# Attention with a running state: folding the state by two parity-scaled ScalarE copies instead of one masked VectorE product

## What is computed

```python
def step(carry, xs):                 # over chunks; q, k after elu+1
    S, z = carry
    qc, kc, vcc = xs
    scores = jnp.einsum('bhid,bhjd->bhij', qc, kc) * mask
    num = jnp.einsum('bhij,bhje->bhie', scores, vcc) + jnp.einsum('bhid,bhde->bhie', qc, S)
    den = scores.sum(-1) + jnp.einsum('bhid,bhd->bhi', qc, z)
    out = num / jnp.clip(den, EPS)[..., None]
    S = S + jnp.einsum('bhjd,bhje->bhde', kc, vcc)
    z = z + kc.sum(2)
...
output = gate * memory_output + (1.0 - gate) * local_output
return x + output @ w_o.T + ffn(xn)
```

## Time and profile before

| | us |
|---|---|
| median of 3 runs | 720.18 |
| lowest and highest | 718.6, 721.35 |
| the profiled execution's own time | 717.36 |
| its span (first to last instruction) | 715.4 |

### The profile page before, as it was taken

The page is one execution under the profiler, slowest core; times in us unless marked ns, Lnnn a source line. Parts: engine busy times, 40 slices in busy tenths (PEclk is TensorE's granted clock), DMA queues, the critical chain, the costliest instruction groups (busy, mean ns, idle before and its releaser), DMA issues. The chain is left out here.

```text
span 715.4 us, 23762 instructions
## 1 busy us (share of the span) xinstructions
PE 616.5 (86%) x8674; PEld 511.4 (71%) x8674; DVE 489.7 (68%) x1317; ACT 349.4 (49%) x870; POOL 309.8 (43%) x401
## 2 busy tenths in 40 slices
PE   1988979979966799999999768888888888988885
PEld 1777868868855699999999756666666666656663
DVE  3565556645683356666666548888888887988886
ACT  4438538547434234444444334555555555555442
POOL 1064083171270820000000033777777776777775
PEclk9999999999988689999999958999999999999997
DMA  8044445345245733333343360222522252323120
GB/s 292 33 140 175 162 148 217 113 170 217 69 169 204 259 104 118 112 121 117 111 124 118 106 227 10 63 92 65 190 88 92 61 212 62 92 62 91 33 62 30
DMA packets 59726, 88.20 MB, mean 123 GB/s; under 512 B 8236, under 2 KB 46348, under 8 KB 58604
## 3 DMA queue, kind: packets, MB, share of 16 engines
q1 hardware_dynamic: 50700, 69.43, 28.8%
q0 software_dynamic: 6656, 16.86, 6.8%
q10 hardware_dynamic: 2272, 0.53, 0.3%
HBM read 46.54 MB, written 40.24 MB: 121 GB/s over the span
## 5 line engine op out<-in xcount | busy, mean ns | idle before, releaser
L1628 POOL TENSOR_TENSOR tick_a<-lane 128x1 f32<-128x1 f32 x32 | 6.3, 196 | 155.4 <-POOLq L826 153.1
L1631 POOL DMA_INDIRECT yg<-d_grouped_y,from_row x64 | 63.3, 990 | 15.5 <-issue 11.6
L87 PE MATMUL e_up<-wb,xb 128*128 x144 | 53.8, 373 | 0.7 <-issue 0.7
L1479 ACT ACTIVATE hid<-a_ring,b 64x128 f32<-64x128 f32 x32 | 11.6, 363 | 87.3 <-remote 50.8
L973 ACT ACTIVATE hb<-e_h 88x256 fp32r<-88x256 f32 x72 | 27.4, 380 | 54.3 <-PE e_h L948 54.3
L1462 ACT ACTIVATE with_mem<-a_ring 128x340 f32<-128x340 f32 x128 | 47.1, 447 | 12.2 <-PE a_ring L1320 12.2
L87 PE MATMUL e_y<-wd,hb 88*128 x146 | 49.3, 338 | 1.6 <-DVE hb L1012 1.6
L1005 DVE TENSOR_TENSOR h_sb<-e_up,silu 128x176 f32<-128x176 f32 x72 | 24.6, 341 | 36.5 <-ACT silu L968 36.5
L813 POOL TENSOR_TENSOR ticks<-lane 128x1 f32<-128x1 f32 x4 | 2.2, 562 | 106.3 <-DVE slot_i L731 106.3
L88 PE MATMUL e_up<-wb,xb 128*128 x144 | 47.5, 330 | 0.0
L89 PE MATMUL e_up<-wb,xb 128*128 x144 | 47.5, 330 | 0.0
(11 more groups left out here) (281 smaller groups left out, 2051.2 us busy)
## 6 DMA issues: line engine op xcount, KB each, us to landing
xg<-d_rows SPq DMA_DIRECT2D x77, 128.0 KB, 2.0
d_grouped_y<-y_sb SPq DMA_DIRECT2D x73, 128.0 KB, 1.8
d_v<-v_half SPq DMA_DIRECT2D x8, 544.0 KB
v<-d_v SPq DMA_DIRECT2D x4, 1088.0 KB, 8.8
d_q<-halves SPq DMA_DIRECT2D x8, 512.0 KB
d_k<-halves SPq DMA_DIRECT2D x8, 512.0 KB
skT<-d_k SPq DMA_DIRECT2D x8, 512.0 KB
total<-d_base SPq DMA_DIRECT2D x8, 512.0 KB
```

What stands on the lines that cost most here:

```text
L87: pe.matmul(out, a[0], b[0], start=start, stop=False)
L1631: pool.indirect_dma_start(yg[tile % GATHERS][:, k, :], None, d["grouped_y"], bass.IndirectOffsetOnAxis(ap=c["from"][:, k, tile:tile + 1], ...
```

## The change

Three things are changed, all in attention. The fold moves from DVE (one product with same_head over 272 columns) to ACT (two copies of 136 columns each, r = 0 and 1, for the even and the odd heads). Each copy is scaled by a column of parity, a table with one number a row that is 1 where the row's head is even (or odd) and 0 elsewhere. This clears the wrong head of each two-by-two block, but not the blocks outside; so the first addition of a batch is now made of the same eight small products as all others, and DVE clears the bank once, before anything else that it does in attention.

```diff
                         of = slice(j * CH, (j + 1) * CH)
-                        if t == 0 and j == 0:
-                            for m in range(KC):
-                                mm = pe.matmul(ps[:, m * HH * HE:(m + 1) * HH * HE], k_tok[of, m * P:(m + 1) * P],
-                                               v_of[of, b % 2, t, m * HH:(m + 1) * HH, :],
-                                               start=(m == 0), stop=True, skip_group_check=True)
-                        else:
...
+                        if (b, t, j) == (0, 0, 0):
+                            pe.wait_ge(s_zero, 1)
+                        for m in range(KC):
+                            for q in range(PP):
+                                at = m * P + 32 * q
+                                first = m * HH + 2 * q
+                                mm = pe.matmul(ps[32 * q:32 * (q + 1), first * HE:(first + 2) * HE],
+                                               k_tok[of, at:at + 32], v_of[of, b % 2, t, first:first + 2, :],
+                                               start=(t == 0 and j == 0 and m == 0), stop=True, skip_group_check=True)
...
+                    if what == "fold":
+                        since(act, ready["state"], b * STATES + 2 * t + j + 1)
+                        since(act, ready["local"], b * NT + t)
+                        of_pairs = "p k (q r e) -> p k q r e"
+                        for r in range(2):
+                            to, of = (x.rearrange(of_pairs, r=2, e=HE)[:, :, :, r, :] for x in (
+                                state[(2 * t + j + 1) % 3][:, :, :],
+                                sums[:, 0:KC * HH * HE].rearrange("p (k n) -> p k n", k=KC)))
+                            ins = act.activation(to, of, ACT.Copy, scale=c["parity"][:, r:r + 1])
+                        ins.then_inc(s_state, 1)
+                        continue
...
             link, links = chain(dve, s_pdve)
+            dve.memset(sums[:, :], 0.0).then_inc(s_zero, 1)
...
-                    elif what == "fold":
-                        since(dve, ready["state"], b * STATES + 2 * t + j + 1)
-                        since(dve, ready["local"], b * NT + t)
-                        dve.tensor_tensor(state[(2 * t + j + 1) % 3][:, :, :].rearrange("p k (h e) -> p k h e", e=HE),
-                                          sums[:, 0:KC * HH * HE].rearrange("p (k h e) -> p k h e", k=KC, e=HE),
-                                          c["same_head"][:, :].unsqueeze(1).unsqueeze(3)
-                                          .broadcast_to([P, KC, HH, HE]), ALU.mult).then_inc(s_state, 1)
```

More of the change, by code:

```diff
@@ L1194, in attention_phase @@
                   "hidden", "values", "local", "gate", "state", "oproj")}
-        s_valT = sem("a_valT")
+        s_valT, s_zero = sem("a_valT"), sem("a_zero")
         s_mask = sem("a_mask")
@@ L1442, in walk @@
                     if what not in ("keys", "outT", "coarseT", "hidden", "values", "gate",
-                                    "mexp", "norms", "rows"):
+                                    "mexp", "norms", "rows", "fold"):
+                        continue
[9 more added lines that the diff above has]
+                        ins.then_inc(s_state, 1)
                         continue
@@ L1513, in walk @@
                     t = n
-                    if what in ("mexp", "coarseT", "keys", "hidden", "outT", "values", "gate", "mask", "rows"):
+                    if what in ("mexp", "coarseT", "keys", "hidden", "outT", "values", "gate", "mask", "rows",
+                                "fold"):
                         continue
```

## The result

The changed kernel takes 722.47 us in the median (718.63 to 728.5, 20 runs); the kernel before, on the same chips, 718.68 (716.54 to 722.14, 20 runs). The ratio is 1.0058, 95% interval 1.0033 to 1.0083: slower by 0.6%, some 4.2 us. (The ratios in this text are not quotients of the medians, which here differ by 3.8.) The profiled execution has a span of 719.8 us against 715.4.

A forecast was written before the change was run, and what follows sets the result against it. With DVE relieved, a chain over ACT, POOL and the indirect DMA was to bind; 6.2 - 1.2 + 1.6 + 0.6 (bank) + 0.2 (end: last round's fold) - 2.6 = 4.8 us on 720.18 gives 725.0, range 708 to 732.

The forecast's parts named there:

- the likeliest case: A chain over ACT, POOL and the indirect DMA sets the round: 725.0 us, range 718 to 732, chance 0.45.
- The copies: Each masked-by-table copy of 136 columns out of PSUM on ACT takes 0.26 us, so 0.52 a fold.
- Where they fall: First fold between hid and with_mem, second between e_t and yg on ACT, 0.52 us each; rn comes 0.52 later.
- the gap of 0.85: Slack in us between the end of ACT's yg and POOL's addition of expert rows, to be used up.
- The link of 1.78: From the end of the first indirect DMA's issue on POOL to ACT's next hid: 1.78 us, an inference.
- The closed chain: From hid through yg, POOL and the indirect DMA to the next hid: 8.97 us a round instead of 8.75.
- a credit of 4 rounds: Rounds where hid starts 0.65 us earlier, right behind the fold's release; 4 x 0.65 = 2.6 us less.
- 6.2 - 1.2 - 2.6: In us: 28 rounds 0.22 longer, 4 rounds without a second fold 0.3 shorter, 4 rounds with early hid 0.65 shorter.
- The dense product: Small products in its place lengthen the first round of three batches by 0.55 us each: 1.6, bounds 0 and 2.6.
- The bank's clearing: DVE clears 512 columns of PSUM on the path to PE's first product: 0.6 us, between 0 and 0.7.
- Faster: Rival: ACT's chain does not close through the indirect DMA, or PE answers hidden earlier; DVE decides, 708 us, chance 0.28.
- Much slower: the masked copies: Rival: in 14 rounds a masked copy behind yg delays attT by about 0.5 us, 7 on top: 732, chance 0.07.

The follow-up runs named there:

- e6_noind_before: The kernel before, with the gathers of expert rows from the fourth tile on replaced by POOL subtractions; ratio 1.0169 to the kernel before.
- e13_dense: The changed kernel with both folds on ACT, but the first product of each batch dense again; ratio 0.9947 to the kernel before.
- e8_early: The changed kernel with the first fold moved ahead of the hidden layer in the order; ratio 0.9959 to the kernel before.

## Why the prediction was right, and where it was not

The sign, the size and the likeliest case held: 725.0 was forecast for 720.18, a factor of 1.0067, and it came to 1.0058. The split of the sum did not hold, and two errors met.

- **The copies** were right: 663.25 to 663.76 is 0.51 a fold, for 0.52. The 0.26 from the rows of hid and e_t was the value; the estimate of 0.30 from the figures of the Trainium skill, page ScalarE: Activation LUTs, section What ACT_TABLE_LOAD costs, was too high here. The bound of 0.8 to 0.9 ns a column was read too low (0.34 us over 340 columns allows 1.0), but the result doesn't hang on it.
- **Where they fall** was right. rn waits 2.35 us for with_mem (over 1.5 was forecast), the gap of 0.85 before POOL's addition is gone, and POOL waits for ACT's yg. In 28 of 30 rounds it begins 0.14 behind yg; 0.05 was taken for this handover.
- **The link of 1.78** was right in kind (e6_noind_before) and wrong as a constant. This is the step that failed. The closed chain was put at 8.97 for all 28 rounds; it is about 9.1 in most rounds with the long link and 8.4 in nine of the ten with a short one. The cause was in the rows: 446.80 in the earlier trace rows has the short link, and I booked it as a credit of 4 rounds, although the chain closing later moves POOL's issue against PE's work in every undisturbed round. I took the two rounds' phases for given. 6.2 - 1.2 - 2.6 and 0.8 for the bank and the end were +3.2; e13_dense measured -3.8.
- **The dense product** was the other failure, +1.6 (bounds 0 and 2.6) where 8 came. The 0.65 of the round at 568.86, taken as 0.55, was near what that round lost (0.82 a batch), but I looked only at that one round. The trace before held a hint of the rest, the pause of 1.23 us at 591.44 and the half-clock stretch behind it, and I gave an upper bound as if only that round could change. How most of the 8 us come about stays open in part, as said above.
- **The bank's clearing** costs 0.39 us on DVE, for 0.6 taken:

```profile
413.17 0.48 DVE L1501 MEMSET a_sums<- 128x512 f32 x1 [2.50 <-PEq L826]
413.56 0.15 DVE L1502 TENSOR_SCALAR half_b<-b 128x1 f32<-128x1 f32 x1
```

- **The rivals.** "Faster" was the better description of the folds alone (rounds of 8.4, and 0.9947 with the dense product), by a mechanism it named as its second condition, an earlier answer of PE. "Much slower: the masked copies" had its mechanism too: 12 of the 14 rounds with a masked copy end with the long link. It costs the gain of these rounds, not 0.5 us on top.

So the right total was luck: -7 in one term and +6 in the other cancelled, and it is weak proof of either.

## What to carry to other kernels

Time a change of several parts in parts: here the half that was to pay (0.9947) and the half that was only its precondition (1.0113) had opposite signs. Work that moves onto a waiting engine belongs ahead of the operation that waits longest, not behind it, if its own input is there sooner: e8_early is faster than both kernels for swapping two items of a list. And a fixed lag read between two engines should be plotted over all rounds before it is used as a constant.

## What the runs showed of the hardware

- While POOL issues two indirect DMAs, PE's result for ACT comes in most rounds 1.1 or 1.8 us after the end of the first issue, even where the second ends later than usual; with the issues gone it comes 0.04 us after PE's record, and also with them when the product right ahead is dense (4 records) rather than 16 small ones.
- PE paused 1.0 to 2.8 us, most often in or beside a product of 16 records, while or just after a load ran at a DMA share of about 1 over 5 us; with the load cut to a share of 0.50 over the same 5 us it did not. A pause of 1.40 us also came at a share of 0.03.
- A product of 256 columns from SBUF takes DVE 0.42 us, and 1.16 us beside POOL's operation of 512 columns.
